# Projection on one NeuronCore: transposes, subtraction and output gate on 64-row tiles of TensorE, with a new order of a unit

## The chip, the cores and the metric

One NeuronCore of a Trainium2 chip runs the whole program. The metric is device time in microseconds; the kernel before took 2902.34 us (median of 3 runs, 2900.99 to 2904.39).

## The reference

The input x is 512 x 512 tokens of 64 channels, float32. Layer 0 is cut here to what the change touches:

```python
xn = ln(group_norm(x))                      # over the 64 channels, then norm_w, norm_b
left  = (xn @ left_w  + left_b)  * mask * sigmoid(xn @ lgate_w + lgate_b)
right = (xn @ right_w + right_b) * mask * sigmoid(xn @ rgate_w + rgate_b)
out_gate = sigmoid(xn @ ogate_w + ogate_b)
out = einsum('bkjd,bkid->bijd', left, right)
x = x + (ln(out) @ out_w + out_b) * out_gate
```

Layer 1 adds to x a product over the 12 lowest Fourier modes of each axis.

## The kernel before

The program is a row of stages, each a block of five instruction streams that meet at its end: `prepare` (statistics, weights), `project` (L382), `contract`, `finish_layer0`, `layer1`. The change lies in `project` alone.

`project` works through 256 units, each of 1,024 tokens: a tile of 128 partitions x 8 tokens x 64 channels (`tile`, L458) in a ring of 4 blocks of 8 units that SyncE loads (L482). For each unit VectorE scales (L635), GpSimd shifts (L507), VectorE measures (L644), GpSimd normalises (L527); once in 8 units VectorE makes a first guess of 1/sqrt (L650 to L661) and GpSimd refines it in three steps (L510). Then the unit goes to TensorE, and the names below are those of the change:

- **Transposes** (L544): 4 matmuls turn two tokens each (a 128 x 128 pair) into `x_ps`, one bank of 512 columns for each of two units. Partitions 0 to 63 then hold the channels of one token of a pair, 64 to 127 those of the other. They signal `turned`.
- ScalarE copies `x_ps` to `high` (L593), rounded to float32r; TensorE adds minus `high` to `x_ps` (`subtract_high`, L553); ScalarE copies what is left to `low` (L598). So a value is carried as high + low.
- **Output gate** (`product` at L558, 128 rows): high x w_high, low x w_high, high x w_low into `o_ps`, 3 matmuls of 128 rows and 512 columns. ScalarE's `gate` (L608) makes the sigmoid and stores it to `gout`.
- **Gates and values** (`both`, L564): the same three products for each half of the partitions, 64 rows each, into the two banks of `g_ps` and of `v_ps`; half 0 and half 1 alternate in the stream. ScalarE's `sigmoid` (L603) writes `sig`, VectorE's `value` (L663) multiplies into `lr`. SyncE stores `lr` and `gout` for each pair of units.

A unit on TensorE is thus 20 matmuls, each with a weight load of its own (LDWEIGHTS): 4 + 1 + 3 of 128 rows, 6 + 6 of 64. The order is written out by hand in the `slot` of each engine: slot n of TensorE (L575) does the transposes of unit n + 2, the subtraction of n + 1, then output gate, gates and values of n. ScalarE (L616): `copy_turned` of n + 2, `copy_rest` of n + 1, `gate` and `sigmoid` of n. VectorE works 18 and 15 units ahead with scale and measure, GpSimd 17, 7 and 5 ahead. `units` (L437) runs slots -lead to 63 unrolled, then a hardware loop of 32 slots for n = 64 to 223, then the last 32 unrolled. In front of each step stand waits on semaphores that count units; a second wait on the same instruction becomes an instruction of its own on that engine.

Of the kernel before, what the change touches and what calls it, by code (L numbers as in the profile page):

```python
# [50 lines left out]
LEAD = 18  # L51
# [330 lines left out]
def project(nc, x, lr_d, gate_d, keep):  # L382
# [5 lines left out]
    with ExitStack() as ctx:  # L388
# [5 lines left out]
        low = [t.sb(f"low{k}", [P, L], F32R) for k in range(2)]  # L394
# [32 lines left out]
        o_in = t.sem("o_in")  # L427
        sig_ready = t.sem("sig_ready")
# [51 lines left out]
        def _(sp):  # L480
# [3 lines left out]
            def slot(n, m, j):  # L484
# [7 lines left out]
                if m % UB == UB - 2:  # L492
                    k = blocks_before(n, m, j, 0) + RING
                    if not (is_int(k) and k >= NBLK):
                        sp.wait_ge(turned, n + 2)
                        load(k, m // UB)
# [7 lines left out]
        def _(pool):  # L504
# [24 lines left out]
            def slot(n, m, j):  # L529
                if (m + 7) % UB < 3:  # L530
                    if inside(n + 7):
                        newton(blocks_before(n, m, j, 7), (m + 7) // UB % 2, (m + 7) % UB)
                if inside(n + 5):
                    normalise(n + 5, m + 5, blocks_before(n, m, j, 5))
                if inside(n + 17):
                    shift(n + 17, m + 17)
# [6 lines left out]
        def _(pe):  # L543
            def transposes(n, m):  # L544
                pe.wait_ge(xn_ready, n + 1)
                at_least(pe, low_ready, n - 1)
                for i in range(RG):
                    pair = tile(m)[:, 2 * i:2 * i + 2, :].rearrange("p t c -> p (t c)")
                    last = pe.matmul(x_ps[m % 2][:, i:L:RG], pair, keep.ident[:, :], start=(i == 0), stop=False,
                                     is_transpose=True, skip_group_check=True)  # L550
                last.then_inc(turned, 1)

            def subtract_high(n, m):  # L553
                pe.wait_ge(high_ready, n + 1)
                pe.matmul(x_ps[m % 2][:, :], keep.minus[:, :], high[m % 4][:, :], start=False, stop=True,
                          skip_group_check=True).then_inc(rest_ready, 1)

            def product(bank, w, m, rows):  # L558
                w_high, w_low = w
                pe.matmul(bank, w_high[rows, :], high[m % 4][rows, :], start=True, stop=False)  # L560
                pe.matmul(bank, w_high[rows, :], low[m % 2][rows, :], start=False, stop=False)
                return pe.matmul(bank, w_low[rows, :], high[m % 4][rows, :], start=False, stop=True)

            def both(bank, w, m):  # L564
                w_high, w_low = w
                halves = [(bank[:, L * e:L * e + L], slice(C * e, C * e + C)) for e in range(2)]
                for out, rows in halves:
                    pe.matmul(out, w_high[rows, :], high[m % 4][rows, :], start=True, stop=False)
                for out, rows in halves:
                    pe.matmul(out, w_high[rows, :], low[m % 2][rows, :], start=False, stop=False)  # L570
                for out, rows in halves:
                    last = pe.matmul(out, w_low[rows, :], high[m % 4][rows, :], start=False, stop=True)  # L572
                return last

            def slot(n, m, j):  # L575
                if inside(n + 2):
                    transposes(n + 2, m + 2)
                if inside(n + 1):
                    subtract_high(n + 1, m + 1)
                if inside(n):  # L580
                    pe.wait_ge(low_ready, n + 1)
# [947 lines left out]
```

## Time and profile before

| what | value |
|---|---|
| runs | 2900.99, 2902.34, 2904.39 us |
| profiled execution, its time | 2902.31 us |
| its span, first to last instruction | 2900.5 us |
| around the span | 1.8 us |
| mean granted TensorE clock | 0.956 |
| stage `project`, first transpose to end of last value | 224.5 to 1076.9 us |
| TensorE busy, VectorE, ScalarE, GpSimd (whole span) | 85%, 76%, 48%, 35% |

The shares of busy time are means over five stages with different limits, so the stage has to be read by itself: stretches of it, what ended the waits in it, and the order of events in one unit. The profile's start of a matmul is the moment it goes to the array; where its weight load is not yet over, the start stands early by the rest of that load. Ends of matmuls are modelled.

### The profile page before, as it was taken

Reading aid. Unit: us, or ns where it says so; the run is one execution under the profiler, and the core shown is the slowest. Engines: PE = TensorE matmul, PEld = TensorE weight load, DVE = VectorE, ACT = ScalarE, POOL = GpSimd, SP = SyncE. Lnnn points to the kernel's source line nnn. Section 1 sums busy time; section 2 is a strip of 40 time slices with the busy share of each in tenths; the row PEclk is TensorE's granted clock in tenths of the full one; section 3 lists DMA queues with packets and bytes.
Section 4 is the critical chain, followed back from the end, with each engine's and each line's share of the span. In section 5 each row is a group of like instructions: output and inputs, shape, how many; then the busy total and the mean of one; then the engine's idle time right before and its main releaser. Section 6 shows DMA issues by size and latency. Waiting matters only on the chain. (4 is left out here: it accounts for less than half of the span.)

```text
span 2900.5 us, 39672 instructions
## 1 busy us (share of the span) xinstructions
PE 2473.0 (85%) x12694; PEld 1847.7 (64%) x12694; DVE 2217.2 (76%) x3468; ACT 1384.5 (48%) x1812; POOL 1020.5 (35%) x1043
## 2 busy tenths in 40 slices
PE   0008999899898988999999999499899999979983
PEld 0005666566565656888888888376666666778872
DVE  6998888778787847888888888777676767527852
ACT  0107888788787875766666666222222222100000
POOL 0019888778787831000000000154444444300000
PEclk9999999999999998999999999799999999959997
DMA  9945999797787866777777776999999999549999
GB/s 384 388 161 206 342 338 340 285 337 285 280 337 288 319 256 255 273 288 275 288 274 286 275 286 247 356 382 416 400 416 400 416 391 398 158 136 370 421 420 411
DMA packets 244939, 926.87 MB, mean 320 GB/s; under 512 B 18009, under 2 KB 21593, under 8 KB 244442
## 3 DMA queue, kind: packets, MB, share of 16 engines
q1 hardware_dynamic: 205912, 796.12, 72.7%
q10 hardware_dynamic: 38898, 129.21, 11.1%
q8 instruction: 60, 0.98, 0.1%
q14 instruction: 69, 0.57, 0.1%
HBM read 527.85 MB, written 394.92 MB: 318 GB/s over the span
## 5 line engine op out<-in xcount | busy, mean ns | idle before, releaser
L1185 POOL TENSOR_TENSOR fi_square_sum<-fi_square_sum,fi_square 128x1024 f32<-128x1024 f32 x128 | 302.9, 2366 | 356.4 <-ACT fi_square L1151 356.4
L864 PE MATMUL ct_acc_ps<-ct_l_hi,ct_r_hi 128*128 128x512 f32 x1024 | 404.8, 395 | 26.7 <-DVE ct_r_lo L941 26.7
L669 DVE SCALAR_TENSOR_TENSOR pj_lr<-pj_v_ps,keep_b_val,pj_sig 128x1024 f32<-128x1024 f32 x256 | 328.7, 1284 | 118.2 <-ACT pj_sig L606 115.3
L865 PE MATMUL ct_acc_ps<-ct_l_lo,ct_r_hi 128*128 128x512 f32 x1024 | 404.5, 395 | 0.0
L866 PE MATMUL ct_acc_ps<-ct_l_hi,ct_r_lo 128*128 128x512 f32 x1024 | 404.4, 395 | 0.0
L1151 ACT ACTIVATE fi_square<-fi_x 128x1024 f32<-128x1024 f32 x128 | 135.5, 1058 | 513.8 <-DVE fi_x L1213 511.3
L507 POOL TENSOR_TENSOR front_ring<-front_ring,front_gn_shift 128x512 f32<-128x512 f32 x256 | 330.9, 1294 | 5.3 <-DVE front_ring L635 5.2
L606 ACT ACTIVATE pj_sig<-pj_g_ps,keep_b_gate 128x1024 f32<-128x1024 f32 x256 | 285.8, 1117 | 42.0 <-PE pj_g_ps L572 36.8
L1106 PE MATMUL fi_y_ps<-fi_scaled,keep_w_bd 128*128 128x512 f32 x512 | 271.9, 613 | 27.4 <-DVE fi_scaled L1196 26.9
L1196 DVE TENSOR_TENSOR fi_scaled<-fi_m,fi_s_ps 128x512 f32<-128x512 f32 x256 | 174.2, 681 | 132.0 <-DMA fi_m<-mixed_d 123.0
L527 POOL TENSOR_TENSOR front_ring<-front_ring,pj_guess 128x512 f32<-128x512 f32 x256 | 267.8, 1047 | 3.3 <-POOL pj_guess L521 1.6
L1177 POOL MEMSET fi_square_sum<- 128x1024 f32 x1 | 1.0, 951 | 759.6 <-POOLq L737 759.6
L1120 PE MATMUL fi_f_ps<-fi_x,fi_basis_rows 128*96 128x256 f32 x1024 | 263.4, 381 | 0.0
L644 DVE BATCH_NORM_STATS2 pj_stats<-front_ring 128x6 f32<-128x128 f32 x1024 | 227.3, 286 | 20.6 <-issue 15.3
L864 PEld LDWEIGHTS ct_acc_ps<-ct_l_hi,ct_r_hi 128*128 128x128 f32 x1024 | 198.3, 194 | 68.6 <-issue 27.1
L1382 PE MATMUL la_ps_ps<-la_col,keep_mask_row 128*128 128x256 f32 x1024 | 226.2, 383 | 16.5 <-DVE la_x L1460 12.5
L1101 PE MATMUL fi_s_ps<-fi_s,fi_pick 128*128 128x512 f32 x256 | 206.9, 809 | 36.0 <-DMA fi_s<-ct_s_low 36.0
L903 ACT ACTIVATE ct_o<-ct_acc_ps 128x512 f32<-128x512 f32 x192 | 113.6, 591 | 238.5 <-PE ct_acc_ps L866 238.5
L1204 DVE SCALAR_TENSOR_TENSOR fi_gated<-fi_y_ps,keep_c_col,fi_g 128x512 f32<-128x512 f32 x256 | 191.4, 748 | 46.5 <-PE fi_y_ps L1106 25.1
L1382 PEld LDWEIGHTS la_ps_ps<-la_col,keep_mask_row 128*128 128x128 f32 x1024 | 196.1, 192 | 46.4 <-DVE la_x L1460 14.5
L866 PEld LDWEIGHTS ct_acc_ps<-ct_l_hi,ct_r_lo 128*128 128x128 f32 x1024 | 198.3, 194 | 41.5
L865 PEld LDWEIGHTS ct_acc_ps<-ct_l_lo,ct_r_hi 128*128 128x128 f32 x1024 | 198.3, 194 | 41.5
(183 smaller groups left out, 5052.3 us busy)
## 6 DMA issues: line engine op xcount, KB each, us to landing
lr_d<-pj_lr SPq DMA_DIRECT2D x128, 1024.0 KB, 5.9
gate_d<-pj_gout SPq DMA_DIRECT2D x128, 512.0 KB, 6.9
ct_l<-lr_d SPq DMA_DIRECT2D x64, 1024.0 KB, 7.0
ct_r<-lr_d SPq DMA_DIRECT2D x64, 1024.0 KB, 9.0
mixed_d<-ct_o SPq DMA_DIRECT2D x64, 1024.0 KB, 5.0
fi_g<-gate_d SPq DMA_DIRECT2D x128, 512.0 KB, 14.6
fi_x<-in_x SPq DMA_DIRECT2D x32, 2048.0 KB, 17.2
fi_m<-mixed_d SPq DMA_DIRECT2D x128, 512.0 KB, 17.6
```

Of the source, the lines that this page charges most:

```text
L507: pool.tensor_tensor(tile(m), tile(m), keep.gn_shift[:, :].unsqueeze(1).to_broadcast([P, WS // 2, C]), ALU.add).then_inc(shifted, 1)
L527: pool.tensor_tensor(tile(m), tile(m), root, ALU.mult).then_inc(xn_ready, 1)
L606: act.activation(sig[m % 2][:, :], g_ps[:, :], ACT.Sigmoid, bias=keep.b_gate[:, 0:1]).then_inc(sig_ready, 1)
L644: last = dve.bn_stats(stats[m // UB % 2][:, RG * (m % UB) + i, :], tile(m)[:, 2 * i:2 * i + 2, :].rearrange("p t c -> p c t"))
L669: dve.scalar_tensor_tensor(out=out[:, :, RG * (m % 2):RG * (m % 2) + RG], in0=v_ps[:, :].rearrange("p (q i) -> p q i", i=RG), scalar=keep. ...
L864: pe.matmul(bank, high, l_hi[b][:, :, k, :], start=(k == 0), stop=False)
L865: pe.matmul(bank, high, l_lo[b][:, :, k, :], start=False, stop=False)
L866: last = pe.matmul(bank, low, l_hi[b][:, :, k, :], start=False, stop=(k == WT - 1))
L1106: pe.matmul(y_ps[n % 2], keep.w2_bd[:, :], scaled[n % 2], start=True, stop=True).then_inc(y_ready, 1)
L1120: last = pe.matmul(f_ps[k % 2], mid.basis_rows[:, s, :], xt[k % XT][:, :, s, :], start=(s == 0), stop=(s == WS - 1))
L1185: pool.tensor_tensor(square_sum[:, :, :], square_sum[:, :, :], square[:, :, :], ALU.add).then_inc(sum_done, 1)
L1382: last = pe.matmul(bank[:, :, s % 2, :], inv_cols[:, s, :], col[:, TG * TILE[n]:TG * TILE[n] + TG, :], start=True, stop=True)
```

## The change

The transposes, the subtraction and the output gate are split into halves e = 0 and e = 1, as gates and values were: half e uses partitions 64e to 64e + 63 as its rows. Four transposes become eight, with 64 columns of the identity as moving operand and a 64 x 128 pair as weights; half e fills columns 256e to 256e + 255 of `x_ps`. One subtraction becomes two, three output gate products become six, each still of 512 columns. A unit has 28 matmuls in place of 20. Both halves of a step now add into one bank, so three new semaphores put half 1 of the transposes and the subtraction ahead of half 0 (`half_turned`, `half_rest`), and half 0 of the output gate ahead of half 1 (`half_o`); TensorE waits for itself there. The transposes run 3 units ahead in place of 2 and the subtraction 2 in place of 1; `low` has 4 buffers in place of 2; all leads of the other engines grow by one unit, and SyncE's load of a block moves one slot. ScalarE's order of a slot becomes `sigmoid` n, `copy_rest` n + 2, `gate` n, `copy_turned` n + 3.

```diff
-LEAD = 18
+LEAD = 19
...
-        low = [t.sb(f"low{k}", [P, L], F32R) for k in range(2)]
+        low = [t.sb(f"low{k}", [P, L], F32R) for k in range(4)]
...
-                if m % UB == UB - 2:
+                if m % UB == UB - 3:
...
-                        sp.wait_ge(turned, n + 2)
+                        sp.wait_ge(turned, n + 3)
                         load(k, m // UB)
...
         @block.tensor
         def _(pe):
...
+            def transposes(n, m, e):
                 for i in range(RG):
+                    pair = tile(m)[side(e), 2 * i:2 * i + 2, :].rearrange("p t c -> p (t c)")
+                    columns = slice(L // 2 * e + i, L // 2 * e + L // 2, RG)
+                    last = pe.matmul(x_ps[m % 2][:, columns], pair, keep.ident[side(e), side(e)],
+                                     start=(e == 1 and i == 0), stop=False, is_transpose=True, skip_group_check=True)
+                last.then_inc(turned if e == 0 else half_turned, 1)
+
+            def subtract_high(n, m, e):
+                if e == 1:
+                    pe.wait_ge(high_ready, n + 1)
+                else:
+                    pe.wait_ge(half_rest, n + 1)
+                last = pe.matmul(x_ps[m % 2][:, :], keep.minus[side(e), :], high[m % 4][side(e), :], start=False,
+                                 stop=(e == 0), skip_group_check=True)
+                last.then_inc(rest_ready if e == 0 else half_rest, 1)
+
+            def one(bank, w, m, e, i, start, stop):
+                weight = w[1 if i == 2 else 0]
+                part = low if i == 1 else high
+                return pe.matmul(bank, weight[side(e), :], part[m % 4][side(e), :], start=start, stop=stop,
+                                 skip_group_check=True)
+
+            def out_gate(n, m, e, i):
+                if e == 0 and i == 0:
+                    at_least(pe, g_done, n)
+                if e == 1 and i == 0:
+                    pe.wait_ge(half_o, n + 1)
...
+                if i == 2:
+                    last.then_inc(o_in if e == 1 else half_o, 1)
...
             def slot(n, m, j):
+                here, ahead, rest = inside(n), inside(n + 3), inside(n + 2)
+                if here:
+                    for i in range(3):
+                        if i == 2 and ahead:
+                            at_least(pe, low_ready, n + 2)
+                        gates(n, m, 0, i)
+                        gates(n, m, 1, i)
+                    if ahead:
+                        pe.wait_ge(xn_ready, n + 4)
+                    out_gate(n, m, 0, 0)
...
+                if ahead:
+                    transposes(n + 3, m + 3, 1)
+                if here:
+                    out_gate(n, m, 0, 1)
+                    out_gate(n, m, 0, 2)
+                if ahead:
+                    pe.wait_ge(half_turned, n + 4)
+                if rest:
+                    subtract_high(n + 2, m + 2, 1)
+                if ahead:
+                    transposes(n + 3, m + 3, 0)
+                if here:
+                    out_gate(n, m, 1, 0)
+                if rest:
+                    subtract_high(n + 2, m + 2, 0)
+                if here:
+                    out_gate(n, m, 1, 1)
+                    values(n, m, 0, 0)
+                    out_gate(n, m, 1, 2)
+                    values(n, m, 0, 1)
+                    values(n, m, 1, 0)
+                    values(n, m, 0, 2)
+                    values(n, m, 1, 1)
+                    values(n, m, 1, 2)
+
+            units(pe, 3, slot)
...
             def slot(n, m, j):
+                if inside(n):
+                    sigmoid(n, m)
                 if inside(n + 2):
+                    copy_rest(n + 2, m + 2)
                 if inside(n):
                     gate(n, m, j)
+                if inside(n + 3):
+                    copy_turned(n + 3, m + 3)
+
+            units(act, 3, slot)
```

`gates(n, m, e, i)` and `values(n, m, e, i)` issue the product i of half e as `both` did, with the waits of before.

## Rows read from the trace of the kernel before

**Rows 1.** The page: busy tenths and granted clock in 40 slices of 72.5 us.
```profile
PE   0008999899898988999999999499899999979983
DVE  6998888778787847888888888777676767527852
ACT  0107888788787875766666666222222222100000
POOL 0019888778787831000000000154444444300000
PEclk9999999999999998999999999799999999959997
```

**Rows 2.** Busy time by engine in stretches of the stage; then clock, DMA share, GB/s.
```profile
300.00:340.00 40.00, 40.00 (x262) 27.28 (x260) 35.55 (x84) 35.85 (x52) 34.41 (x44) 1.00 0.92 323
540.00:580.00 40.00, 34.03 (x204) 23.07 (x206) 30.49 (x72) 26.95 (x40) 29.08 (x42) 0.87 0.65 241
1020.00:1060.00 40.00, 40.00 (x260) 27.53 (x260) 19.95 (x30) 35.85 (x53) 19.30 (x28) 1.00 0.62 246
```

**Rows 3.** Who waited for whom, 230 to 1040 us: total us, times, longest.
```profile
POOL pj_guess_sq L515 <- DVE pj_guess L660: 113.6, 30, 11.8
DVE pj_lr L669 <- ACT pj_sig L606: 94.4, 193, 2.7
PEld pj_g_ps L568 <- issue: 90.9, 244, 0.7
ACT pj_high L596 <- PE pj_x_ps L549: 86.3, 242, 11.0
PEld pj_x_ps L549 <- issue: 82.0, 228, 0.4
...
PE pj_v_ps L568 <- DVE pj_lr L669: 38.5, 5, 9.4
ACT pj_sig L606 <- PE pj_g_ps L572: 34.8, 203, 0.9
DVE front_ring L635 <- issue: 21.6, 4, 5.5
```

**Rows 4.** Timeline of one unit, matmuls: start, us, engine, line, operation.
```profile
602.27 0.66 PE L549 MATMUL pj_x_ps<-keep_ident,front_ring 128*128 128x128 f32 x4
602.68 0.47 PE L555 MATMUL pj_x_ps<-pj_high,front_minus 128*128 128x512 f32 x1
603.00 0.39 PE L560 MATMUL pj_o_ps<-pj_high,front_w_og_high 128*128 128x512 f32 x1
603.23 0.40 PE L561 MATMUL pj_o_ps<-pj_low,front_w_og_high 128*128 128x512 f32 x1
603.46 0.40 PE L562 MATMUL pj_o_ps<-pj_high,front_w_og_low 128*128 128x512 f32 x1
603.78 0.50 PE L568 MATMUL pj_g_ps<-pj_high,front_w_gate_high 64*128 64x512 f32 x2
604.12 0.39 PE L570 MATMUL pj_g_ps<-pj_low,front_w_gate_high 64*128 64x512 f32 x2
604.35 0.39 PE L572 MATMUL pj_g_ps<-pj_high,front_w_gate_low 64*128 64x512 f32 x2
604.59 0.39 PE L568 MATMUL pj_v_ps<-pj_high,front_w_val_high 64*128 64x512 f32 x2
604.81 0.39 PE L570 MATMUL pj_v_ps<-pj_low,front_w_val_high 64*128 64x512 f32 x2
605.04 0.40 PE L572 MATMUL pj_v_ps<-pj_high,front_w_val_low 64*128 64x512 f32 x2
605.37 0.33 PE L549 MATMUL pj_x_ps<-keep_ident,front_ring 128*128 128x128 f32 x1
```

**Rows 5.** The same unit, ScalarE.
```profile
602.96 0.60 ACT L596 ACTIVATE pj_high<-pj_x_ps 128x512 fp32r<-128x512 f32 x1 [0.16 <-PE pj_x_ps L549]
603.46 0.59 ACT L601 ACTIVATE pj_low<-pj_x_ps 128x512 fp32r<-128x512 f32 x1
603.93 0.69 ACT L613 ACTIVATE pj_gout<-pj_o_ps,keep_b_out 128x512 f32<-128x512 f32 x1
604.79 1.12 ACT L606 ACTIVATE pj_sig<-pj_g_ps,keep_b_gate 128x1024 f32<-128x1024 f32 x1 [0.16 <-PE pj_g_ps L572]
606.06 0.60 ACT L596 ACTIVATE pj_high<-pj_x_ps 128x512 fp32r<-128x512 f32 x1 [0.15 <-PE pj_x_ps L549]
```

**Rows 6.** The same unit, weight loads (PEld).
```profile
602.66 0.19 PEld L555 LDWEIGHTS pj_x_ps<-pj_high,front_minus 128*128 128x128 f32 x1
602.77 0.19 PEld L560 LDWEIGHTS pj_o_ps<-pj_high,front_w_og_high 128*128 128x128 f32 x1
...
603.78 0.19 PEld L568 LDWEIGHTS pj_g_ps<-pj_high,front_w_gate_high 64*128 64x128 f32 x2 [0.37 <-issue]
603.89 0.19 PEld L570 LDWEIGHTS pj_g_ps<-pj_low,front_w_gate_high 64*128 64x128 f32 x2
604.12 0.18 PEld L572 LDWEIGHTS pj_g_ps<-pj_high,front_w_gate_low 64*128 64x128 f32 x2
```

**Rows 7.** Eight full transposes in a later stage, one group (timeline).
```profile
1965.58 1.06 PE L1112 MATMUL fi_z_ps<-keep_ident,fi_gated 128*128 128x128 f32 x8
```

**Rows 8.** Small matmuls of the last stage: durations ns, first and last start us.
```profile
L1357 PEld LDWEIGHTS la_ps_ps<-la_xm,la_w x288: 184/203/205, 2552.7 to 2584.3; 128*64 128x64 f32 x144
```

**Rows 9.** Busy times and granted clock (third number from the end) there.
```profile
2553.00:2584.00 31.00, 31.00 (x284) 31.00 (x283) 0.00 (x0) 0.00 (x0) 0.00 (x0) 0.50 0.53 213
```

**Rows 10.** The transposes over the whole stage: durations ns min/median/max.
```profile
L549 PE MATMUL pj_x_ps<-keep_ident,front_ring x1024: 272/273/477, 224.5 to 1067.0; 128*128 128x128 f32 x171
```

**Rows 11.** Timeline: a value product that VectorE releases.
```profile
236.79 1.27 DVE L669 SCALAR_TENSOR_TENSOR pj_lr<-pj_v_ps,keep_b_val,pj_sig 128x1024 f32<-128x1024 f32 x1
238.12 0.19 PEld L568 LDWEIGHTS pj_v_ps<-pj_high,front_w_val_high 64*128 64x128 f32 x2 [1.65 <-DVE pj_lr L669]
```

**Rows 12.** GpSimd while the stage fills (timeline).
```profile
225.61 1.04 POOL L527 TENSOR_TENSOR front_ring<-front_ring,pj_guess 128x512 f32<-128x512 f32 x1
226.61 1.27 POOL L507 TENSOR_TENSOR front_ring<-front_ring,front_gn_shift 128x512 f32<-128x512 f32 x1
227.84 1.04 POOL L527 TENSOR_TENSOR front_ring<-front_ring,pj_guess 128x512 f32<-128x512 f32 x1
```

More of the change, by code:

```diff
@@ L427, in project @@
         o_in = t.sem("o_in")
+        half_turned = t.sem("half_turned")
+        half_rest = t.sem("half_rest")
+        half_o = t.sem("half_o")
         sig_ready = t.sem("sig_ready")
@@ L543, in _, with side @@
         def _(pe):
-            def transposes(n, m):
-                pe.wait_ge(xn_ready, n + 1)
-                at_least(pe, low_ready, n - 1)
+            def side(e):
+                return slice(C * e, C * e + C)
+            def transposes(n, m, e):
                 for i in range(RG):
[L548 to L573, printed above, removed]
@@ L575, in slot @@
-            def slot(n, m, j):
[L576 to L581, printed above, removed]
-                    at_least(pe, g_done, n)
-                    product(o_ps[:, :], keep.w_og, m, slice(0, P)).then_inc(o_in, 1)
-                    at_least(pe, sig_ready, n)
-                    both(g_ps, keep.w_gate, m).then_inc(gates_in, 1)
-                    at_least(pe, gated, n)
-                    both(v_ps, keep.w_val, m).then_inc(vals_in, 1)
@@ L589, in _ @@
-            units(pe, 2, slot)
+                    pair = tile(m)[side(e), 2 * i:2 * i + 2, :].rearrange("p t c -> p (t c)")
[11 more added lines that the diff above has]
+                last.then_inc(rest_ready if e == 0 else half_rest, 1)
@@ new lines, in one @@
+            def one(bank, w, m, e, i, start, stop):
[8 more added lines that the diff above has]
+                    pe.wait_ge(half_o, n + 1)
+                last = one(o_ps[:, :], keep.w_og, m, e, i, e == 0 and i == 0, e == 1 and i == 2)
+                if i == 2:
+                    last.then_inc(o_in if e == 1 else half_o, 1)
@@ new lines, in gates, with values @@
+            def gates(n, m, e, i):
+                if e == 0 and i == 0:
+                    pe.wait_ge(low_ready, n + 1)
+                    at_least(pe, sig_ready, n)
+                last = one(g_ps[:, L * e:L * e + L], keep.w_gate, m, e, i, i == 0, i == 2)
+                if e == 1 and i == 2:
+                    last.then_inc(gates_in, 1)
+            def values(n, m, e, i):
+                if e == 0 and i == 0:
+                    at_least(pe, gated, n)
+                last = one(v_ps[:, L * e:L * e + L], keep.w_val, m, e, i, i == 0, i == 2)
+                if e == 1 and i == 2:
+                    last.then_inc(vals_in, 1)
@@ L599, in copy_rest @@
                 act.wait_ge(rest_ready, n + 1)
-                at_least(act, vals_in, n - 1)
-                act.activation(low[m % 2][:, :], x_ps[m % 2][:, :], ACT.Copy).then_inc(low_ready, 1)
+                at_least(act, vals_in, n - 3)
+                act.activation(low[m % 4][:, :], x_ps[m % 2][:, :], ACT.Copy).then_inc(low_ready, 1)
             def sigmoid(n, m):
@@ L616, in slot @@
             def slot(n, m, j):
+                if inside(n):
+                    sigmoid(n, m)
                 if inside(n + 2):
-                    copy_turned(n + 2, m + 2)
-                if inside(n + 1):
-                    copy_rest(n + 1, m + 1)
+                    copy_rest(n + 2, m + 2)
                 if inside(n):
                     gate(n, m, j)
-                    sigmoid(n, m)
-            units(act, 2, slot)
+                if inside(n + 3):
+                    copy_turned(n + 3, m + 3)
+            units(act, 3, slot)
         @block.vector
```

29 lines of the change are left out of this document (16 added, 13 removed).

## The prediction

> **What bounds the kernel now.** First the page: in slices 4 to 15, the stage `project`, TensorE stands at 9 tenths nearly throughout, VectorE, ScalarE and GpSimd at 7 to 9 [rows 1]. Busy tenths don't say who paces, so next come stretches: in 40 us TensorE is busy for 40.00, ScalarE for 35.85, VectorE for 35.55, GpSimd for 34.41, and at the end of the stage, where VectorE and GpSimd have only half their work left, TensorE issues as many matmuls as before (260 against 262) [rows 2]. So neither of those two sets the pace. Then the waits: ScalarE waits for TensorE 242 and 203 times, VectorE for ScalarE's `sigmoid` 193 times, while TensorE's only waits for another engine's data that matter are 5, of up to 9.4 us, behind VectorE; its gaps in front of weight loads are put to "issue", 0.3 to 0.4 us, twice a unit [rows 3]. The long ones are the edges of the hardware loop, where VectorE fetches its code (4 times, 5.5 us the longest part); the change touches them little, and I cost them at nothing.
>
> Last the timeline of one unit [rows 4]. It lasts 605.37 - 602.27 = 3.10 us, and it adds up without any wait for another engine:
> - Ten times 0.23 us, the distance between matmuls of 512 columns that follow each other (604.12 to 605.04 is 4 x 0.23): subtraction, three output gate products, six pairs of halves. A pair of 64-row matmuls takes the same 0.23 as one of 128 rows; its halves run side by side. 2.30.
> - Four times 0.11 us for the transposes. Eight in a row elsewhere span 1.06, the last being 0.27: 0.79 / 7 = 0.11 [rows 7, 10]. 0.44.
> - 0.36 for the two changes between 128 and 64 rows: 603.46 to 603.78 is 0.32, not 0.23 (0.09 more); the first gate products then wait for their weights (603.78 to 604.12 is 0.34: 0.11 more, the 0.11 between loads of [rows 6]); 605.04 to 605.37 is 0.33 (0.10 more); and the five loads from 602.27 to 602.77 take 0.50, 0.06 over 4 x 0.11 [rows 6].
>
> The sum is 3.10. TensorE's own stream is the bound. Close behind it: ScalarE idles 0.16 twice in a unit, so its own need is 2.78 [rows 5]; VectorE's idle of 94.4 us over 193 waits, 0.4 to 0.5 a unit, leaves it some 2.7.
>
> **What the change removes.** All 28 matmuls of a unit are now of 64 rows, so the 0.36 goes: 3.10 - 0.36 = 2.74 if each half could go its own way: ten matmuls of 0.23 and four transposes of 0.11 for each half. That the transposes are halves does not make them cheaper: their moving operand has 64 columns, but the weights still have 128. Two rows bound one of them. From above, 0.11, the distance of two loads of 64 x 128 weights in [rows 6]. From below, 0.055: loads of 64 columns come every (2584.3 - 2552.7) / 287 = 0.11 us at a granted clock of 0.50 [rows 8, 9], thus 0.055 at full clock; so a load goes by its columns. I take 0.11, since the columns stay 128.
>
> The Trainium skill ("TensorEngine Tiling (Array Packing)", Key Properties) says that a change of tiling mode drains TensorE. By that rule alone the unit would come down by the whole 0.36. The trace agrees with the drain, 0.09 and 0.10 us in front of the two changes.
>
> **What it adds.** TensorE has one stream. The halves now do different things at a time, so it matters whether a matmul that can't start yet holds back the ones behind it that belong to the other half. In the pairs of today nothing can show this: both start together [rows 4]. I take it that starts keep the order of the stream. Walk from the first transpose of half 1 (0.00), 512-column matmuls at 0.23, transposes at 0.11:
> - transposes of half 1 at 0.00, 0.11, 0.22, 0.33. The second output gate product of half 0 stands behind them and starts at 0.33, though its half has been free since about 0.05; the third at 0.56.
> - half 0's transposes follow at 0.79, 0.90, 1.01, 1.12. Output gate product 0 of half 1 stands behind them: 1.12.
> - half 1 then has three output gate products (1.12, 1.35, 1.58), three values (1.81, 2.04, 2.27), and in the next slot three gates (2.50, 2.73, 2.96). The next transposes of half 1 start at 3.19.
>
> The loop is 6 x 0.11 + 11 x 0.23 = 0.66 + 2.53 = 3.19 us, 0.09 more than now. Half 0 has 0.45 of idle time in it, half 1 as much.
>
> **The new waits.** A wait is passed on in about 0.05 us (value ends 236.79 + 1.27 = 238.06, the load starts at 238.12 [rows 11]); add 0.11 for the load. A matmul of 512 columns is done 0.39 after its start [rows 4], a transpose 0.27 [rows 10].
> - `half_turned`: 0.33 + 0.27 + 0.16 = 0.76 for the subtraction of half 1; half 0's transposes, queued behind it, start at 0.79 anyway. Slack 0.03.
> - `half_o`: 0.56 + 0.39 + 0.16 = 1.11 against 1.12. Slack 0.01.
> - `half_rest`: 0.76 + 0.39 + 0.16 = 1.31 for the subtraction of half 0; behind it output gate 1 of half 1 at 1.35. Slack 0.04.
>
> All three fit, barely. Cost nothing in the sum; above, 0.10 us a unit if a hand-over takes 0.1 more than I think. Below, nothing, since the loop does not run through them.
>
> **The other engines.** ScalarE: the subtraction is ready at 1.31 + 0.39 = 1.70; copy_rest, gate and copy_turned follow, each 0.47 to 0.6 apart or 0.69 [rows 5], and `high` is there by about 3.5, where half 1's next subtraction needs it at 3.84. sigmoid then runs to 4.6, before the next copy_rest at 4.9. Its need of 2.78 is covered by 3.19. If TensorE fell below 2.78, ScalarE would pace. `low` in four buffers takes away the wait for `vals_in` one unit back: nothing, for nobody waited there. VectorE and GpSimd have the same work, one unit earlier. SyncE's load of a block stays behind the same stores, one slot sooner and with its condition met sooner: nothing; DMA queues see the same 1 MB a unit. The eight more matmuls and loads a unit are code to fetch at the loop's edges, under VectorE's stall there.
>
> **Filling the stage.** One more unit is turned ahead, and GpSimd supplies a unit in 227.84 - 225.61 = 2.2 us then [rows 12]. At most 2.2, at least 0; I take 1.5.
>
> **The sum.** 250 of 256 units at this pace x 0.09 = 22.5, plus 1.5 = 24. Against the profiled execution (2902.31 us, of which 2900.5 is the span; 0.03 below the median of the runs) this gives 2926 us. About 0.2%, 5.8 us, is what a measurement of this kernel can tell from no change.
>
> **Rivals.**
> - *The halves go independently* (faster). Then a blocked matmul holds up only its own half. Half 1 needs 2.74 plus what `half_turned` costs it: the subtraction starts 0.27 + 0.16 = 0.43 after the last transpose, not 0.11: 3.06. Hence -0.04 a unit, to -0.07 if the hand-over is quicker: some -14 us, with the filling 2890. For it: halves do run side by side. Against it: in 256 units no matmul starts ahead of one before it in the stream. It decides as soon as more than 0.09 of the 0.45 idle goes. Chance 0.22.
> - *Transposes with half the columns are cheaper*, 0.06 in place of 0.11, starts in order. The loop saves 0.30, but the next matmul still waits 0.11 for its load after each group of four, and the subtractions' waits then bind: 3.05 to 3.08. About -9 us, 2895, at the edge of what can be told. Against it: the load of 128 columns. Chance 0.14.
> - *A transpose does not run beside a matmul of the other half.* The transposes wait for output gate product 0 (0.04), product 1 for the last one's end (0.05), half 0's transposes for the subtraction's end (0.2), product 0 of half 1 for theirs (0.05): 3.19 + 0.34 at most, 3.4 with what overlaps. +0.3 x 250 = 75, 2979. No row has the two side by side. Chance 0.10.
> - *The 0.36 is no price of changing rows* and stays in part. For: "issue" names no cause. Then the unit is at 3.1 to 3.3. Chance 0.04.
>
> The Trainium skill ("TensorE: Matmul & The Clock Gate", Part 3, The mechanism) has matmuls in strict order of the program at start and end, and only weight loads pulled ahead. No run here shows it yet; by it the first rival falls and the loop of 3.19 stands.
>
> **How the numbers follow.** Forecast 0.50, of which 0.04 within 0.2%, then 0.22, 0.14, 0.10, 0.04. Faster: the first rival and 0.08 of the second, 0.30. Within 0.2%: 0.04 + 0.06 + 0.02 = 0.12. Slower: 0.46 + 0.10 + 0.02 = 0.58. The range reaches down to both of the first rivals (2885, 0.07 a unit less) and up to the forecast with every hand-over 0.1 later and some of the third rival (3.33 a unit, +0.23 x 250 + 1.5 = 59: 2961).
>
> **What would show it.** The distance from unit to unit on TensorE: 3.19, against 3.10. In the timeline, output gate 1 of half 0 starts with the last transpose of half 1, and 0.3 us after the first; no gap of 0.36 from "issue" is left; transposes of a half 0.11 apart. ScalarE and VectorE wait 0.1 longer a unit than now. Wrong if product 1 starts before the last transpose of half 1 (the first rival), if transposes come every 0.06 (the second), or if the subtraction of half 1 and the transposes of half 0 start over 0.05 later than walked (a hand-over dearer than 0.16).

## The result, and the profile after

The changed kernel takes 2877.27 us (median of 4 runs, 2873.93 to 2879.03), the kernel before 2903.36 us beside it (4 runs, 2900.99 to 2905.66): ratio 0.9904, 95% interval 0.9892 to 0.9915. It is 26 us faster. The forecast was 2926 us, 24 us slower, and the range ended at 2885. Medians here leave out slow runs; there was one, of 6859.69 us, among the four of the kernel that issues half transposes twice. The profiled execution took 2879.03 us, of which 2877.2 is the span.

The page after answers to [rows 1]:

```profile
PE   0008999889989969999999999599998999979983
DVE  6998999779779848888888888777676767427852
ACT  0107999779779966676766766122221222100000
POOL 0019988788788820000000000244443444300000
```

The busy tenths of the stage look the same; it only ends sooner. The same stretch as in [rows 2], and one at the end of the stage:

```profile
300.00:340.00 40.00, 40.00 (x371) 35.94 (x372) 36.63 (x87) 36.56 (x54) 35.50 (x47) 1.00 0.95 336
1000.00:1040.00 40.00, 40.00 (x370) 36.13 (x368) 17.43 (x14) 36.75 (x54) 13.33 (x21) 1.00 0.64 254
```

TensorE's records cover all 40 us again, but a record covers it also while one half stands idle: so here busy is no sign of a bound. ScalarE does 36.56 in place of 35.85, VectorE 36.63 in place of 35.55: all do the same units 2 to 3% faster. From the first stretch to the second VectorE and GpSimd lose more than half of their work and TensorE's pace stays, 371 and 370 matmuls, so they don't set it.

The unit is measured from start to start of VectorE's `value` in the trace: a median of 3.10 us before and 3.02 after. The stage (first transpose to end of last value) goes from 224.5 to 1076.9 down to 224.2 to 1048.7, from 852.4 to 824.5 us, 28 less. 255 units x 0.08 make 21 of it. The long steps at the edges of the hardware loop come to 46 us over a unit's pace before (seven steps, 5.1 to 13.1) and 38 after (four, 12.1 to 13.3), 8 more; the filling gives 1.4 back, since the first value starts at 237.9 and not at 236.8. The rest of the program lies within its scatter: from the first matmul of `contract` to the end it takes 1798 us before, 1803 after, and 1798 to 1803 in the runs below, whose `contract` is the same.

Who waited for whom, 230 to 1020 us, answers to [rows 3]:

```profile
DVE pj_lr L717 <- PE pj_v_ps L570: 80.9, 105, 10.6
ACT pj_low L648 <- PE pj_x_ps L563: 62.3, 248, 2.0
POOL pj_guess_sq L518 <- DVE pj_guess L708: 56.0, 30, 3.5
ACT pj_sig L653 <- PE pj_g_ps L570: 36.3, 7, 8.7
PEld pj_g_ps L570 <- issue: 31.4, 4, 8.1
```

The gaps put to "issue" twice a unit are gone; what is left of them is the four edges of the loop. ScalarE now waits in each unit for one thing, the subtraction (L563), 0.25 us each time (62.3 / 248). The unit itself, matmuls:

```profile
607.92 0.39 PE L570 MATMUL pj_g_ps<-pj_high,front_w_gate_high 64*128 64x512 f32 x1
607.94 0.38 PE L570 MATMUL pj_v_ps<-pj_high,front_w_val_low 64*128 64x512 f32 x1
...
608.63 0.39 PE L570 MATMUL pj_g_ps<-pj_high,front_w_gate_low 64*128 64x512 f32 x1
608.75 0.47 PE L570 MATMUL pj_o_ps<-pj_high,front_w_og_high 64*128 64x512 f32 x1
608.87 0.41 PE L554 MATMUL pj_x_ps<-keep_ident,front_ring 64*128 64x64 f32 x4
609.06 0.39 PE L570 MATMUL pj_o_ps<-pj_low,front_w_og_high 64*128 64x512 f32 x1
609.29 0.39 PE L570 MATMUL pj_o_ps<-pj_high,front_w_og_low 64*128 64x512 f32 x1
609.33 0.49 PE L563 MATMUL pj_x_ps<-pj_high,front_minus 64*128 64x512 f32 x1
609.52 0.40 PE L554 MATMUL pj_x_ps<-keep_ident,front_ring 64*128 64x64 f32 x4
609.74 0.50 PE L570 MATMUL pj_o_ps<-pj_high,front_w_og_high 64*128 64x512 f32 x1
609.88 0.50 PE L563 MATMUL pj_x_ps<-pj_high,front_minus 64*128 64x512 f32 x1
610.08 0.39 PE L570 MATMUL pj_o_ps<-pj_low,front_w_og_high 64*128 64x512 f32 x1
...
610.97 0.39 PE L570 MATMUL pj_g_ps<-pj_high,front_w_gate_high 64*128 64x512 f32 x1
610.98 0.39 PE L570 MATMUL pj_v_ps<-pj_high,front_w_val_low 64*128 64x512 f32 x1
...
611.66 0.39 PE L570 MATMUL pj_g_ps<-pj_high,front_w_gate_low 64*128 64x512 f32 x1
...
611.90 0.34 PE L554 MATMUL pj_x_ps<-keep_ident,front_ring 64*128 64x64 f32 x3
```

Three things stand in it.

- **Halves pass each other.** The first gate product of half 0 (607.92) starts ahead of the last value product of half 1 (607.94), which stands ahead of it in the program. It is so again one unit on (610.97, 610.98). Where it waits for nothing, each half goes on every 0.23 us by itself.
- **Four half transposes and the end of the last take 0.41 us**, of which the last is 0.22: (0.41 - 0.22) / 3 = 0.06 apart, not 0.11. The whole stage, to be laid beside [rows 10]:

```profile
L554 PEld LDWEIGHTS pj_x_ps<-keep_ident,front_ring x2048: 134/138/226, 224.2 to 1037.1; 64*128 64x128 f32 x187
L554 PE MATMUL pj_x_ps<-keep_ident,front_ring x2048: 213/222/367, 224.2 to 1037.2; 64*128 64x64 f32 x187
```

- **A loop through ScalarE and both halves sets the pace.** The same unit on ScalarE, to be laid beside [rows 5]:

```profile
607.91 0.69 ACT L660 ACTIVATE pj_gout<-pj_o_ps,keep_b_out 128x512 f32<-128x512 f32 x1
608.49 0.60 ACT L643 ACTIVATE pj_high<-pj_x_ps 128x512 fp32r<-128x512 f32 x1
609.06 1.12 ACT L653 ACTIVATE pj_sig<-pj_g_ps,keep_b_gate 128x1024 f32<-128x1024 f32 x1
610.41 0.60 ACT L648 ACTIVATE pj_low<-pj_x_ps 128x512 fp32r<-128x512 f32 x1 [0.23 <-PE pj_x_ps L563]
610.91 0.68 ACT L660 ACTIVATE pj_gout<-pj_o_ps,keep_b_out 128x512 f32<-128x512 f32 x1
```

and three of its weight loads:

```profile
608.72 0.18 PEld L570 LDWEIGHTS pj_o_ps<-pj_high,front_w_og_high 64*128 64x128 f32 x1
608.75 0.26 PEld L554 LDWEIGHTS pj_x_ps<-keep_ident,front_ring 64*128 64x128 f32 x2
...
609.33 0.18 PEld L563 LDWEIGHTS pj_x_ps<-pj_high,front_minus 64*128 64x128 f32 x1
```

The loop is walked in two parts, and it takes two units.

1. From ScalarE through half 0 to half 1: `gate` ends at 607.91 + 0.69 = 608.60. The load of output gate product 0 of half 0, which waits for its `g_done`, starts at 608.72, products 1 and 2 start at 609.06 and 609.29. Product 2 is done at 609.68 and signals `half_o`; output gate product 0 of half 1 starts at 609.74. Its load lies bare, so product 1 follows 0.34 later, at 610.08, and the last gate product at 611.66. Then half 1 is free for the transposes of the next unit: they start at 611.90. That is 3.30 us.
2. From the transposes back to ScalarE, told for the unit shown, since the steps behind 611.90 are the same one unit on: transposes of half 1 from 608.87, the last done at 609.28 (608.87 + 0.41); subtraction of half 1 from 609.33, done at 609.82; subtraction of half 0 from 609.88, done at 610.38; `copy_rest` at 610.41, `gate` 0.50 behind it, done at 611.59. That is 2.72 us.

Together 6.02 us for two units, 3.01 a unit. The trace also holds the moment of each signal, and in 209 units away from the loop's edges these links hold with hardly any scatter (from the 5th to the 95th of 100): output gate product 0 starts 0.135 us after `g_done` (0.135 to 0.135), the first product of half 1 0.043 after `half_o` (0.043 to 0.046), each subtraction 0.043 after its signal (0.043 to 0.044), `copy_rest` 0.022 after its own (0.022 to 0.023). The transposes of half 1 are not held up by `g_done`, though they stand behind it in the program: they start 0.00 us after half 1 is free, and anywhere from 0.23 to 0.35 after `g_done`. Half 1's own stream is nearly as long as the loop: without `half_o` its first output gate product could follow the subtraction at 609.33 + 0.34 = 609.67, 0.07 sooner (0.05 in the median).

### The profile page after: what moved, and what is told of

It is laid out like the page before. It is cut to its first block and busy times, and to the rows that moved or that the text cites. A ratio compares the mean times of both kernels' runs of the same rounds, so it can differ in the third digit from the quotient of the medians.

```text
span 2877.2 us, 44035 instructions
## 1 busy us (share of the span) xinstructions
PE 2459.1 (85%) x14742; PEld 2000.9 (70%) x14742; DVE 2216.7 (77%) x3468; ACT 1380.9 (48%) x1812; POOL 1021.6 (36%) x1043
## 5 line engine op out<-in xcount | busy, mean ns | idle before, releaser
L563 PE MATMUL pj_x_ps<-pj_high,front_minus 64*128 64x512 f32 x512 | 257.6, 503 | 0.2
L570 PE MATMUL pj_o_ps<-pj_high,front_w_og_high 64*128 64x512 f32 x512 | 249.4, 487 | 0.1
L554 PE MATMUL pj_x_ps<-keep_ident,front_ring 64*128 64x64 f32 x2048 | 209.8, 223 | 25.5 <-POOL front_ring L530 24.7
L554 PEld LDWEIGHTS pj_x_ps<-keep_ident,front_ring 64*128 64x128 f32 x2048 | 204.3, 140 | 34.2 <-POOL front_ring L530 25.0
```

The lines of the kernel that those rows point to most:

```text
L554: last = pe.matmul(x_ps[m % 2][:, columns], pair, keep.ident[side(e), side(e)], start=(e == 1 and i == 0), stop=False, is_transpose=True, ...
```

## The experiments

Three questions: what the 0.36 us of a unit was, in what order the halves really start and signal, and what sets 3.02. Ratios are to the kernel before, on the same chip; "unit" is always the median from `value` to `value`.

### What the 0.36 us was

**Two more changes of rows.** In the kernel before, gates go ahead of the output gate, so that a unit changes between 128 and 64 rows four times, not twice:

```diff
-                    at_least(pe, g_done, n)
-                    product(o_ps[:, :], keep.w_og, m, slice(0, P)).then_inc(o_in, 1)
                     at_least(pe, sig_ready, n)
                     both(g_ps, keep.w_gate, m).then_inc(gates_in, 1)
+                    at_least(pe, g_done, n)
+                    product(o_ps[:, :], keep.w_og, m, slice(0, P)).then_inc(o_in, 1)
```

ScalarE's `sigmoid` goes ahead of `gate` likewise.

> The kernel before, with the output gate put between gates and values (and ScalarE's gate after its sigmoid): the same 20 matmuls a unit, but four changes between 128 and 64 rows in place of two. Theory (a change of rows costs a drain of about 0.10 us and leaves the next load of 0.11 exposed): about 0.4 us a unit more, unit 3.5 us, some +100 us. Rival (the 0.36 us of "issue" has another cause, such as the start of a slot): unit stays at 3.10, no change.

3001.11 us, 1.0341 (1.0324 to 1.0359), unit 3.52. The timeline of it:

```profile
603.02 0.39 PE L572 MATMUL pj_g_ps<-pj_high,front_w_gate_low 64*128 64x512 f32 x2
603.35 0.50 PE L560 MATMUL pj_o_ps<-pj_high,front_w_og_high 128*128 128x512 f32 x1
603.69 0.39 PE L561 MATMUL pj_o_ps<-pj_low,front_w_og_high 128*128 128x512 f32 x1
603.92 0.40 PE L562 MATMUL pj_o_ps<-pj_high,front_w_og_low 128*128 128x512 f32 x1
604.24 0.50 PE L568 MATMUL pj_v_ps<-pj_high,front_w_val_high 64*128 64x512 f32 x2
```

At each of the changes shown 0.32 or 0.33 in place of 0.23, and then 0.34 for the load that could not go ahead: 0.21 a change, 0.42 for two. The accounting of [rows 4] holds, and the wait put to "issue" is a price of changing rows.

**The order alone.** The changed kernel's order, leads and buffers, with transposes, subtraction and output gate left at 128 rows:

```diff
-                    transposes(n + 3, m + 3, 1)
+                    transposes(n + 3, m + 3)
                 if here:
-                    out_gate(n, m, 0, 1)
-                    out_gate(n, m, 0, 2)
-                if ahead:
-                    pe.wait_ge(half_turned, n + 4)
+                    out_gate(n, m, 1)
+                    out_gate(n, m, 2)
```

> The changed kernel's order, leads, buffers and ScalarE order, but transposes, subtraction and output gate on 128 rows as before (no waits between halves). Theory (the gain comes from dropping the two changes of rows): unit at 3.10 us as before, no change against the kernel before. Rival (the gain comes from the new order and the longer lead): unit about 3.02, some -25 us.

2898.62 us, 0.9987 (0.9977 to 0.9996), unit 3.145. The order is worth nothing in a unit, 0.04 the wrong way; the long steps at the loop's edges come to 27 us over the pace, 19 less than before, and that makes up for it.

**The halves alone.** The kernel before with its order, and the three steps in halves, one half after the other:

```diff
+                    transposes(n + 2, m + 2, 1)
+                    pe.wait_ge(half_turned, n + 3)
                 if inside(n + 1):
-                    subtract_high(n + 1, m + 1)
+                    subtract_high(n + 1, m + 1, 1)
...
+                    for e in range(2):
+                        for i in range(3):
+                            out_gate(n, m, e, i)
```

> The kernel before in its old order and leads, but transposes, subtraction and output gate in halves with the three hand-overs; the halves follow each other directly. Theory (hand-overs cost 0.5 us after each 512-column matmul unless other work lies between, and one half's chain T1, S1, S0, og0, og1, gates, values is then in series): unit 4.0 to 4.5 us, +230 to +350 us. Rival (hand-overs are cheap and dropping the row changes is what counts): unit at most 3.1.

3227.36 us in a single run, unit 4.44. With the halves and without the new order the kernel would be 11% slower: the pieces of the two halves stand one behind the other, each with a wait and a bare load in front of it (subtractions at 606.74 and 607.29, output gate products 0 at 607.63 and 608.54), and half 1 idles some 1.4 us between its subtraction and its output gate. Neither part does it alone. The gain is what halves save, on the condition that the order gives one half work while the other waits. Halves save two things, the changes of rows and (below) time in the transposes; no run has one of them without the other.

### In what order halves start, and in what order they signal

**Values of half 0 ahead of the output gate of half 1.** In the changed kernel:

```diff
-                    out_gate(n, m, 1, 1)
                     values(n, m, 0, 0)
-                    out_gate(n, m, 1, 2)
                     values(n, m, 0, 1)
-                    values(n, m, 1, 0)
                     values(n, m, 0, 2)
+                    out_gate(n, m, 1, 1)
+                    out_gate(n, m, 1, 2)
+                    values(n, m, 1, 0)
```

> The changed kernel, the end of a slot not interleaved: three values of half 0, then output gate 1 and 2 of half 1, then the values of half 1. Theory A (a matmul that can't start holds back only those of its own half): unit stays within 0.03 of 3.02 us, no change. Theory B, that of the prediction (starts keep the order of the stream): output gate 1 of half 1 waits for value 2 of half 0, 2 x 0.23 = 0.46 us a unit more, some +110 us.

2915.49 us, 1.0043 (1.0029 to 1.0057), unit 3.19: neither of the two. The timeline, TensorE:

```profile
605.68 0.39 PE L570 MATMUL pj_o_ps<-pj_low,front_w_og_high 64*128 64x512 f32 x1
605.79 0.39 PE L570 MATMUL pj_v_ps<-pj_high,front_w_val_high 64*128 64x512 f32 x1
605.90 0.39 PE L570 MATMUL pj_o_ps<-pj_high,front_w_og_low 64*128 64x512 f32 x1
606.02 0.39 PE L570 MATMUL pj_v_ps<-pj_low,front_w_val_high 64*128 64x512 f32 x1
...
606.25 0.39 PE L570 MATMUL pj_v_ps<-pj_high,front_w_val_low 64*128 64x512 f32 x1
```

and ScalarE:

```profile
605.99 0.60 ACT L648 ACTIVATE pj_low<-pj_x_ps 128x512 fp32r<-128x512 f32 x1 [0.29 <-PE pj_x_ps L563]
606.70 0.69 ACT L660 ACTIVATE pj_gout<-pj_o_ps,keep_b_out 128x512 f32<-128x512 f32 x1
```

The starts are free: output gate product 1 of half 1 (605.68) goes ahead of value product 0 of half 0 (605.79), and product 2 (605.90) ahead of values 1 and 2, though all three values stand ahead of both. But ScalarE's `gate` needs product 2, which ends at 605.90 + 0.39 = 606.29, and starts only at 606.70; `copy_rest` would have let it start at 606.49. What ends just before is value product 2 of half 0: 606.25 + 0.39 = 606.64. So a matmul that passed others signals only when those ahead of it in the program are done. The signals' own times in the trace say the same: in 208 units between 300 and 1000 us, `o_in` comes a median 0.38 us after the recorded end of product 2, and 0.031 (0.030 to 0.032) after that of value product 2 of half 0.

**The same with one value less ahead.** This tells late signals from a harm in the order itself: now value 2 of half 0 stands behind output gate product 2 of half 1, values 0 and 1 ahead of product 1.

```diff
-                    out_gate(n, m, 1, 1)
                     values(n, m, 0, 0)
-                    out_gate(n, m, 1, 2)
                     values(n, m, 0, 1)
-                    values(n, m, 1, 0)
+                    out_gate(n, m, 1, 1)
+                    out_gate(n, m, 1, 2)
                     values(n, m, 0, 2)
+                    values(n, m, 1, 0)
```

> As e4_halves_in_blocks, but output gate 1 and 2 of half 1 stand behind two values of half 0, not three. Theory (halves start independently, but ends are reported in program order, so o_in comes with the end of the value ahead of it): o_in comes 0.23 us sooner than in e4, after which it hardly binds: unit 3.02 to 3.06. Rival (starts keep the order of the stream): 0.23 us a unit over the changed kernel, 3.25. Rival (e4's loss has nothing to do with order of ends): as e4, 3.19.

2878.57 us, 0.9918 (0.9902 to 0.9935), unit 3.02, the pace of the changed kernel. The 37 us between the two are the late signal.

**Transposes ahead of the output gate.** If halves were wholly free, output gate product 0 would lose nothing by standing behind the four transposes of half 1, and these would no longer stand behind the wait for `g_done`:

```diff
+                        if i == 2 and ahead:
+                            pe.wait_ge(xn_ready, n + 4)
                         gates(n, m, 1, i)
-                    if ahead:
-                        pe.wait_ge(xn_ready, n + 4)
-                    out_gate(n, m, 0, 0)
...
                     transposes(n + 3, m + 3, 1)
                 if here:
+                    out_gate(n, m, 0, 0)
                     out_gate(n, m, 0, 1)
```

> The changed kernel with the four transposes of half 1 moved ahead of output gate 0, so that they no longer stand behind its wait for ScalarE's gate (g_done). Theory (the unit of 3.02 us is a loop through g_done, output gate 0, transposes, the two subtractions, copy_rest and gate; a matmul reports its end only after those ahead of it in the program): the subtraction of half 1 still stands behind the three output gate products and reports after them, so only a little goes, unit 2.97 to 3.00 us, -5 to -12 us against the changed kernel. Rival (the loop ends with the transposes' place): 2.8 to 2.9 us. Rival (TensorE's stream is the bound, not the loop): no change.

2917.3 us, 1.0061 (1.0044 to 1.0078), unit 3.20: a gain was expected, and it lost 40 us against the changed kernel. The timeline:

```profile
604.15 0.69 ACT L660 ACTIVATE pj_gout<-pj_o_ps,keep_b_out 128x512 f32<-128x512 f32 x1
...
604.60 0.39 PE L570 MATMUL pj_g_ps<-pj_high,front_w_gate_low 64*128 64x512 f32 x1
...
605.02 0.39 PE L570 MATMUL pj_g_ps<-pj_high,front_w_gate_low 64*128 64x512 f32 x1
...
605.25 0.21 PE L554 MATMUL pj_x_ps<-keep_ident,front_ring 64*128 64x64 f32 x1
605.26 0.18 PEld L570 LDWEIGHTS pj_o_ps<-pj_high,front_w_og_high 64*128 64x128 f32 x1
```

Half 0 is free at 604.60 + 0.23 = 604.83 and `g_done` is there at 604.84, but the load of output gate product 0 starts at 605.26, once the first transpose of half 1 has started. From 605.02, when the last gate product of half 1 starts, it is the fifth matmul in line of those that have not started; at 605.25 it becomes the fourth. Nor was there anything to gain: the transposes start when half 1 is free (605.02 + 0.23), as they do in the changed kernel. What changed is the start of output gate product 0, a median 0.43 us after `g_done` and not 0.135: 0.3 us more in a loop of two units is 0.15 a unit, most of the 0.18 measured.

**Three of the four ahead.** If it is such a reach, one transpose moved behind output gate product 0 undoes the loss:

```diff
-                    out_gate(n, m, 0, 0)
...
-                    transposes(n + 3, m + 3, 1)
+                    transposes(n + 3, m + 3, 1, range(3))
+                if here:
+                    out_gate(n, m, 0, 0)
+                if ahead:
+                    transposes(n + 3, m + 3, 1, range(3, RG))
```

> As e3_transposes_first (unit 3.20 us, 40 us slower than the changed kernel), but only three of the four transposes of half 1 stand ahead of output gate 0, the fourth behind it. Theory (an instruction of one half passes blocked ones of the other only over a short reach: in e3 seven stood between it and the head, here five): output gate 0 passes again, unit 2.97 to 3.02 us, some 45 us faster than e3. Rival (e3 lost because transposes ahead of the output gate are bad as such, or because starts keep the order after all): 3.15 to 3.20, as e3.

2870.12 us, 0.9886 (0.9871 to 0.9902), unit 2.99:

```profile
604.90 0.39 PE L571 MATMUL pj_g_ps<-pj_high,front_w_gate_low 64*128 64x512 f32 x1
604.91 0.50 PE L571 MATMUL pj_o_ps<-pj_high,front_w_og_high 64*128 64x512 f32 x1
605.13 0.28 PE L554 MATMUL pj_x_ps<-keep_ident,front_ring 64*128 64x64 f32 x2
```

The product (604.91) goes ahead of three transposes (the first at 605.13) that stand ahead of it, as the fourth in line. One transpose further back cost 47 us. The run is also 5 us faster than the changed kernel beside it (2875.15 us, below): output gate product 0 starts 0.044 us after `g_done` here; why not 0.135 is open. Whether the limit counts matmuls, or loads too, these two runs don't tell. The other traces agree with it: with the starts of the changed kernel and its variants (nine traces, 64,798 matmuls past 240 us) laid beside the order of the program, 1,247 went as the third in line, 1,036 as the fourth, and none from further back.

### What a transpose costs

**Half transposes twice.** The changed kernel, with the four transposes of half 1 issued twice over and those of half 0 once; the extra four repeat the same work.

```diff
             def transposes(n, m, e):
-                for i in range(RG):
+                for i in [*range(RG), *range(RG)][0 if e == 1 else RG:]:
```

> The changed kernel with the four transposes of half 1 issued twice in a row (the second time over the first, same result). Theory (a transpose of 64 rows and 64 columns costs 0.06 us and stands in the loop that bounds the unit): 4 x 0.06 = 0.24 us more, less what overlaps output gate 0: unit 3.20 to 3.26 us, +45 to +60 us against the changed kernel. Rival (0.11 us each, as the prediction had it): +0.40 to +0.44 us, +100 us or more. Rival (not in the loop): no change.

2927.63 us (three runs), 1.0083 (1.0063 to 1.0103), unit 3.21.

**Full transposes twice**, in the kernel before, again as repeated work:

```diff
-                for i in range(RG):
+                for i in [*range(RG), *range(RG)]:
```

> The kernel before with its four full transposes of a unit issued twice (the second time over the first, same result). Theory (a full transpose costs 0.11 us, twice that of a half one in e13_transposes_twice): 4 x 0.11 = 0.44 us a unit more, unit 3.54, some +110 us. Rival (full ones too cost 0.06): +0.24 us, +60 us.

3006.03 us, 1.0352 (1.0335 to 1.0369), unit 3.54. Four more full transposes cost 0.44 a unit, 0.11 each, as [rows 7] have it. Four more of half 1 cost 0.19, but that is no price of four transposes: they start 0.06 apart in that run too, and the way from the first to the subtraction of half 1 grows from 0.46 to 0.71 us, by 0.25. The rest had been slack in half 1's own stream, which now is the loop. So a half transpose takes some 0.06, little over half of a full one, and a unit spends 0.24 on each half where it spent 0.44 on both at once.

### What sets 3.02

**The subtraction ahead of the transposes.** The transposes of half 1 stand in the loop that sets the pace, ahead of both subtractions; so they have to leave it. In this order both subtractions go as soon as `high` allows, the transposes of half 1 between them and those of half 0 near the end of the slot; within the reach of four and with signals in mind:

```diff
                     out_gate(n, m, 0, 0)
...
+                    out_gate(n, m, 0, 1)
+                if rest:
+                    subtract_high(n + 2, m + 2, 1)
+                if here:
+                    out_gate(n, m, 0, 2)
                 if ahead:
                     transposes(n + 3, m + 3, 1)
+                if rest:
+                    subtract_high(n + 2, m + 2, 0)
                 if here:
-                    out_gate(n, m, 0, 1)
-                    out_gate(n, m, 0, 2)
+                    out_gate(n, m, 1, 0)
+                    values(n, m, 0, 0)
                 if ahead:
                     pe.wait_ge(half_turned, n + 4)
-                if rest:
-                    subtract_high(n + 2, m + 2, 1)
...
                 if ahead:
                     transposes(n + 3, m + 3, 0)
                 if here:
...
                     values(n, m, 1, 2)
```

The gate and value products around them, and the waits for `xn_ready` and `low_ready`, shift too.

> The changed kernel's instructions and waits in another order: the subtraction of half 1 right behind output gate 1 and ahead of the transposes, the subtraction of half 0 behind the transposes of half 1, and the transposes of half 0 at the end of the slot. Theory (the loop through ScalarE bounds the unit): the transposes leave the loop, unit 2.85 to 2.90 us, some -35 us against the changed kernel, near 2840 us; then ScalarE's own 2.78 is next. Rival (TensorE's stream bounds it: the same 28 matmuls): unit stays at 3.02.

2859.33 us, 0.9854 (0.9836 to 0.9872), unit 2.91: just above the 2.85 to 2.90 expected, and the total some 19 us short of what was hoped for. The total, 18 us under that of the changed kernel, is half of the 35 expected. Run again beside the changed kernel:

> The changed kernel itself, unchanged, beside e8_again on one chip: 26 us faster than the kernel before, as measured.

> e8_subtraction_first again, more rounds, beside the changed kernel: 15 to 20 us faster than after_again, ratio to the kernel before 0.984 to 0.987. If the gain was chance, within 5 us of after_again.

2875.15 us (0.9904, 0.9889 to 0.9919) for the changed kernel, 2857.94 us (0.9846, 0.9832 to 0.9859) for this one, 17 us less and 45 us under the kernel before: it is the best version here. Its waits:

```profile
ACT pj_sig L654 <- PE pj_g_ps L570: 77.7, 231, 8.1
DVE pj_lr L718 <- PE pj_v_ps L570: 77.3, 122, 9.7
...
ACT pj_low L649 <- PE pj_x_ps L563: 3.7, 5, 1.8
```

ScalarE's wait for the subtraction, 248 times after, is down to 5; now `sigmoid` waits for the gates, 231 times. What sets 2.91 was not tried. Why the total gains less than 0.11 x 255 = 28: the mean of a unit is 2.96, not 2.91. In a row of eight steps one is long, 3.40 beside 2.87 to 2.96; it is the one in which VectorE also makes the first guess, and at this pace it does not catch up.

## Why the prediction was wrong

- **The accounting of the unit before was right**: 2.30 + 0.44 + 0.36. The run with two more changes of rows measured 0.21 a change, and the gaps that held the 0.36 went. Only its last 0.06 is read off wrongly: five loads in 0.50 us are not slow. It stands in the matmuls, 602.27 to 603.00 being 0.73 against 0.44 + 0.23.
- **"I take it that starts keep the order of the stream"**: this is the step that failed, and the forecast hung on it. The rows of before, in which the halves always start together, could not show it either way. After, the halves pass each other (607.92 ahead of 607.94). In-order starts, with transposes of 0.11, would have given 3.19. The Trainium skill ("TensorE: Matmul & The Clock Gate", Part 3, The mechanism) has matmuls in strict order at start and end. For ends the runs agree, as far as signals show them (`o_in` 0.38 us behind the product's end, 37 us in the total); for starts the measurement decides against it.
- **"I take 0.11, since the columns stay 128"**: mis-sized, 0.06. The bound from above was the distance of loads for products, where a load of 64 rows is recorded at 183 ns; for a half transpose it is 138. That record does not explain the drop: a full transpose's load is recorded at 140 and comes every 0.11. The bound from below, 0.055, lay near the true value. Transposes' matmuls shrink, from 273 to 222 ns with 64 in place of 128 moving columns, 51 ns, as much as their distance (0.109 to 0.061). That points to the moving columns, but 64 rows with 128 columns, or 128 rows with 64, wasn't tried.
- **The rivals**: the two faster ones were held apart, each in the place of the other, and were both true. Together they give for half 1, with a last transpose of 0.22, 3 x 0.06 + 0.22 + 0.16 + 10 x 0.23 = 2.86, which the prediction didn't price. Measured was 3.02. That the sum of the first rival lies near it (3.06, 2890 us) is in part luck: too much for transposes stands there against too little for `half_o`. That transposes don't run beside products of the other half (0.10) is refuted: product 1 of half 0 starts at 609.06 as the transposes of half 1 run from 608.87.
- **"All three fit, barely. Cost nothing"**: this failed too. The sizes of a hand-over were right, 0.05 for the wait (609.28 to 609.33) and 0.11 for the load. But what each wait was to hide behind was work of the other half; with free starts there is none, and all three stand in the loop, 0.043 us behind their signals in every unit. What lies between 2.86 and 3.02 stands at `half_o`: output gate product 0 of half 1 waits for it some 0.05, and then has its load bare, 0.11 (609.74 to 610.08 is 0.34, not 0.23). And `half_o` hangs on `g_done`, thus on ScalarE. The walk checked each new wait for its slack on TensorE, and not the way round through ScalarE; ScalarE was looked at for its need of 2.78 only, not for its latency.
- **The filling was right**, 1.5 said, 1.4 measured. **The loop's edges, costed at nothing**, gave 8 us. The run with the order alone has them 19 us lower than before; but the run with halves alone, in the old order and leads and at a slower pace, has them lower by 15 too (31 us). So the cause is open.
- **The drain**: the Trainium skill ("TensorEngine Tiling (Array Packing)", Key Properties) says that a change of tiling mode drains TensorE. The run with two more changes agrees, 0.10 at each, and adds 0.11 for the load behind it.

## What to carry to other kernels

Where two row tiles of TensorE work side by side, write the stream so that neighbours belong to different tiles and what unblocks another engine does not stand behind a long piece of the other tile: starts pass each other only over a short reach, and signals not at all. Once TensorE's own stream has slack, trace the way round through the other engines (who signals whom until the same step comes again) and take out of that loop what need not be in it; it can take more than one unit to close. Here, an order with the transposes out of it was worth 17 us. A layout that avoids a change of rows is only as good as the order that gives one tile work while the other waits.

## What the runs showed of the hardware

- Matmuls on different row tiles start out of program order, when their own tile is free: the fourth in line of those not started went (604.91), the fifth did not (605.02 to 605.25), nor did any from further back than the fourth in nine traces.
- They signal in program order: a product signalled 0.38 us after its own recorded end, and 0.031 after that of the product ahead of it in the program.
- A change between 128 and 64 rows costs 0.21 us: a gap of 0.10 and 0.11 of load laid bare.
- Transposes of 64 rows with 64 moving columns start 0.06 us apart, full ones 0.11; a load of 64 x 128 is recorded at 138 ns for a transpose and 183 for a product.
